# One broadcast DMA in place of two for the rows of B and C of the third channel tile

## What is computed

```python
xz = u @ W_in                                  # 96 -> 2*192 channels
xr, z = split(xz)
x = silu(causal_conv(xr, conv_w) + conv_b)     # 192 channels, 4 taps
dt, B, C = split(x @ W_x)                      # 6 + 16 + 16 columns
delta = softplus(dt @ W_dt + b_dt)
# for every channel d and every state n of 16, along time t:
#   h[t] = exp(delta[t, d] * A[d, n]) * h[t-1] + delta[t, d] * x[t, d] * B[t, n]
#   y[t, d] = sum over n of h[t] * C[t, n]
y = (y + x * D) * silu(z)
out = y @ W_out
```

## Time and profile before

| | before |
|---|---|
| median of 3 runs | 2131.67 us (2131.48 to 2132.75) |
| the profiled execution | 2132.49 us |
| its span, first to last instruction | 2130.5 us |
| GpSimd (POOL) busy | 1938.7 us, 91% |
| VectorE (DVE) busy | 1829.3 us, 86% |
| TensorE (PE) busy | 1819.0 us, 85%, at a mean granted clock of 0.944 |
| DMA | 415.01 MB, the packets of its one busy queue take 64.5% of 16 engines' span |

### The profile page before, as it was taken

One profiled execution on the slowest core, in us unless ns is written; L12 is line 12 of the kernel. 1 busy time (PEld: TensorE's weight loads), 2 busy tenths in 40 slices (PEclk: granted clock), 3 DMA queues, 4 the chain that ended last, 5 costly groups with the idle time before them and its releaser, 6 DMA issues. The chain is left out here.

```text
span 2130.5 us, 16128 instructions
## 1 busy us (share of the span) xinstructions
PE 1819.0 (85%) x4474; PEld 699.1 (33%) x4474; DVE 1829.3 (86%) x1110; ACT 1163.3 (55%) x1206; POOL 1938.7 (91%) x852
## 2 busy tenths in 40 slices
PE   5798789798899899789889889879989988987777
PEld 2233233333333333233333323323333333333322
DVE  2889887877799997997898997998889999799994
ACT  2756464655755745735655744744575574453331
POOL 0999989797899999999999999899899999999996
PEclk9799899999999999999999999999999999989997
DMA  3667556555566776775675785676566677667673
GB/s 83 206 222 185 188 179 189 156 202 189 143 208 204 206 221 205 198 216 191 192 207 197 218 208 204 219 194 211 172 193 208 204 203 217 215 201 213 223 211 94
DMA packets 124454, 415.01 MB, mean 195 GB/s; under 512 B 18556, under 2 KB 22924, under 8 KB 124364
## 3 DMA queue, kind: packets, MB, share of 16 engines
q1 hardware_dynamic: 124364, 413.98, 64.5%
HBM read 403.48 MB, written 6.29 MB: 192 GB/s over the span
## 5 line engine op out<-in xcount | busy, mean ns | idle before, releaser
L861 POOL TENSOR_TENSOR ring<-ring,c_ring 128x1024 f32<-128x1024 f32 x576 | 1344.4, 2355 | 116.9 <-DVE ring L817 104.5
L495 PE MATMUL y_ps<-ring,wp 128*128 128x512 f32 x2304 | 1184.6, 629 | 79.5 <-POOL ring L861 51.0
L817 DVE TENSOR_TENSOR_SCAN ring<-a_ring,b_ps 128x1024 f32<-128x1024 f32 x392 | 895.6, 2285 | 34.1 <-ACT a_ring L624 2.5
L495 PEld LDWEIGHTS y_ps<-ring,wp 128*128 128x128 f32 x2304 | 445.2, 199 | 574.4 <-issue 387.2
L817 DVE TENSOR_TENSOR_SCAN ring<-b_ps,b_ring 128x1024 f32<-128x1024 f32 x184 | 416.6, 2272 | 52.1 <-POOL b_ring L855 24.0
L784 DVE TENSOR_TENSOR b_ps<-u_ab,b_ps 128x1024 f32<-128x1024 f32 x240 | 291.1, 1213 | 101.1 <-PE b_ps L483 88.9
L624 ACT ACTIVATE a_ring<-delta_ab,wp 128x1024 f32<-128x1024 f32 x240 | 271.8, 1140 | 176.9 <-DVE ring L817 176.3
L855 POOL TENSOR_TENSOR b_ring<-u_ab,b_ring 128x1024 f32<-128x1024 f32 x144 | 339.2, 2355 | 0.1
L617 ACT ACT_TABLE_LOAD x186 | 238.6, 1283 | 84.6 <-PE bank L518 36.4
L624 ACT ACTIVATE b_ps<-delta_ab,wp 128x1024 f32<-128x1024 f32 x144 | 160.4, 1115 | 221.2 <-DVE ring L817 220.7
L624 ACT ACTIVATE a_ring<-delta_m,wp 128x1024 f32<-128x1024 f32 x152 | 173.6, 1143 | 152.0 <-DVE ring L817 151.7
(11 more groups left out here) (75 smaller groups left out, 930.4 us busy)
## 6 DMA issues: line engine op xcount, KB each, us to landing
c_ring<-c_rows SPq DMA_DIRECT2D x384, 512.0 KB, 4.4
c_ring<-c_rows SPq DMA_DIRECT2D x384, 256.0 KB, 4.2
b_ring<-b_rows SPq DMA_DIRECT2D x144, 512.0 KB, 5.6
b_ring<-b_rows SPq DMA_DIRECT2D x80, 256.0 KB, 5.3
out<-io SPq DMA_DIRECT2D x16, 192.0 KB, 3.1
io<-x SPq DMA_DIRECT2D x6, 384.0 KB, 6.7
b_in<-parts SPq DMA_DIRECT2D x36, 64.0 KB, 2.1
dt_in<-parts SPq DMA_DIRECT2D x72, 24.0 KB
```

The source lines that it names most:

```text
L495: nc.tensor.matmul(half(y_ps[:, :], j), ident, half(ring[:, g % RING, :], j), start=(n == 0), stop=(n == NS - 1)).then_inc(g_summed, 1)
L817: nc.vector.tensor_tensor_scan(out=h, data0=a, data1=b, initial=0.0, op0=ALU.mult, op1=ALU.add).then_inc(h_ready, 1)
L861: nc.gpsimd.tensor_tensor(r, r, c_ring[:, g % C_RING, :], ALU.mult).then_inc(g_ready, 1)
```

## The change

For the third tile a single `dma_start` takes both batches' rows. Its source is `rows[:, n:n+1, :]` broadcast to the shape [2, 64, 1024], its destination the slot's 128 partitions. Tiles 0 and 1 keep their DMA. The counts on which GpSimd waits fall to 16 per use everywhere.

```diff
-        dmas = lambda g: 2 if g % STEPS // NS == 2 else 1
-        c_uses, spread = [], [0] * C_RING
-        for g in range(ALL_STEPS):
-            spread[g % C_RING] += dmas(g)
-            c_uses.append(16 * spread[g % C_RING])
-        b_uses, spread = {}, [0] * B_RING
-        for m, g in enumerate(pool_steps):
-            spread[m % B_RING] += dmas(g)
-            b_uses[g] = 16 * spread[m % B_RING]
+        c_uses = [16 * (g // C_RING + 1) for g in range(ALL_STEPS)]
+        b_uses = {g: 16 * (m // B_RING + 1) for m, g in enumerate(pool_steps)}
...
             def spread_row(dst, rows, k, n, landed_in):
-                if k < 2:
-                    sp.dma_start(dst, rows[k, n:n + 1, :].to_broadcast([P, T])).then_inc(landed_in, 16)
-                    return
-                for b in range(2):
-                    sp.dma_start(dst[b * DM:(b + 1) * DM, :],
-                                 rows[b, n:n + 1, :].to_broadcast([DM, T])).then_inc(landed_in, 16)
+                src = rows[k, n:n + 1, :].to_broadcast([P, T]) if k < 2 else rows[:, n:n + 1, :].to_broadcast([2, DM, T])
+                sp.dma_start(dst, src).then_inc(landed_in, 16)
```

## The result

| | before | after |
|---|---|---|
| median | 2132.21 us (4 runs) | 3812.28 us (3810.03 to 3819.13, 4 runs) |
| ratio | | 1.7884, 95% interval 1.7853 to 1.7915 |
| span of the profiled execution | 2130.5 us | 3817.3 us |
| twelve third-tile stretches | 760.1 us | 2444.5 us |
| all the rest of the span | 1370.4 us | 1372.8 us |

A stretch is counted as in the prediction, here from GpSimd's timeline: from the end of the product of step 28 to the end of that of step 47. The last three rows are of the two profiled executions (2132.49 and 3819.13 us). Of the 1687 us by which the spans differ, 1684 lie in the stretches; the other parts of the kernel keep their time within 2.4 us.

What follows compares the result with a forecast made beforehand. GpSimd, busy 91% of the span, bounds the kernel before; then two DMA engines pace the third tiles. 2132 + 1687 (232 DMAs at 10.54 us, 2445, less 758) + 35 = 3854, said as 3850 us; range 3600 to 4500.

Steps and rivals of the forecast that it cites:

- The mechanism: Third-tile DMAs: division by outermost dimension, here 2, puts each 512 KB DMA on two fixed engines, 64 rows each; chance 0.80.
- The step that was an extension of the rows: For a DMA whose two sides differ in outermost count, the smaller count decides the engines, here two of 16.
- The price of a row: 4 KB on one engine with a full queue takes 164.7 ns, so a third-tile DMA takes 10.54 us.
- The ends of a stretch: After each of twelve third-tile stretches, landing and last product add 4.4 us, 52 us in all, cancelled against B's earlier issue.
- The time before: The twelve third-tile stretches of the kernel before the change take 758 us in all.
- The small ones: Late `dt_in` loads in item 1 add about 15 us, TensorE's lower clock after the stretches 20 us: 35 us.
- The waits: GpSimd's wait for rows of C grows from 9.1 us to over 1400 us.
- No change: Rival: all 16 engines serve the merged third-tile DMAs, time 2132 us, +-4; chance 0.08.
- faster: Rival: all 16 engines are used and earlier landings remove C waits, -9.1 us at most, 2123 us; chance 0.03.
- The slow price of 271 ns: Rival: two engines, each 4 KB row at the unsaturated stretch's 271 ns, 4024 us in place of 2445, total 5430 us; chance 0.05.
- Rotating pairs: Rival: third-tile DMAs in flight on different engine pairs, about 3 us each, some 2150 to 2500 us; more engines, chance 0.04.

Runs made afterwards that it cites:

- e1: Changed kernel, third-tile rows read from HBM copies, each row 8 times (outermost dimension 16), the item's eight copy writes issued together: 2201.82 us, ratio 1.0329.
- e2: As e1, but with each row 4 times in the HBM copy, so an outermost dimension of 8: 2303.04 us.
- e3: As e1, but with each row twice in the HBM copy, so an outermost dimension of 4: 2664.1 us, ratio 1.2501.
- e7: Changed kernel with each third-tile row as two DMAs, one per half of the time axis, each with outermost dimension 2: 3930.34 us.
- e8: As e1, but with the eight writes of the copies issued one per step over eight steps: 2133.01 us, ratio 0.9994.
- e9: Kernel with only B's third-tile rows merged (2415.19 us), those rows issued nine steps ahead in place of six: 2409.51 us.
- e10: As e2, but with the copies 5 KB apart in HBM in place of 4 KB: 2245.42 us.

## Why the prediction was right

It said 3850 us, the median is 3812; it said +1687 us for the stretches, the trace has +1684.

- **The mechanism.** Right: 11,596 signals, share 0.13, 52 GB/s, and e1, e2 and e3 set the number of engines by the outermost count, with the third tile's bytes the same; e7 brings back the number of DMAs and leaves the engines at two, and the time stays. The step that was an extension of the rows (that the smaller of two unequal counts decides) is now shown for 2, 4, 8 and 16. That the merged rows share one fixed pair is shown by the share of 0.13 with three or four DMAs in flight, 34 us from issue to product ("30 us or more" was predicted).
- **The price of a row.** I took the saturated 164.7 ns; it is 158.9 ns, 10.17 us a DMA and not 10.54, 4% less, and between the two best rows.
- **The ends of a stretch.** Here an error was hidden. 232 x 10.17 = 2359 us, and the stretches take 2444.5, so their ends add 85 us, 7 us each in the mean (some 12 us in a `FWD` item, 1 to 7 in the others); I had set +52 for landing and last product against B's head start and let them cancel. The smaller price and the larger ends offset each other (-86 and +85), so that the sum of 2445 came out to the microsecond by luck. By kind: `FWD` items take 195 to 196 us (190 predicted), `ROWS` 194 to 200 (200), `BWD` 216 to 221 (221).
- **The time before.** 758 us predicted, 760.1 counted.
- **The small ones.** The 35 us for the `dt_in` chain of item 1 and for TensorE's clock are not there: outside the stretches the kernel takes 2.4 us more. The loads of `dt_in` are late as predicted (at 672.6 us TensorE has waited 27.9 us for one), but the first u of the next item is started 2.75 us after GpSimd's last product, where it was 1.00 us before, so the chain costs some 2 us and not 15. TensorE does run at a lower level in the stretches (0.54 granted from 1120 to 1280 us, and 753 ns a matmul at line 484 over the whole kernel against 629 for the same ones before), but no time is lost by it outside the stretches. These terms were wrong, and they are nearly all of the difference between the 3854 worked out and the 3819.13 us of the profiled execution.
- **The waits.** "Over 1400 us" for C: 1417.6, and 250.1 for B, which I had not priced apart. What I had not foreseen is that SyncE's issues themselves are held.
- **The rivals.** No change and faster: both wanted 16 engines, the signals exclude it; e8 shows that on 16 engines "no change" would have been the right one of the two (2133.01, no gain from the 9.1 us of waits). The slow price of 271 ns: not for two engines, so the choice between the two rows was right. The reason given for it, that the row holds pauses, does not hold up: with sixteen engines busy at a share of 0.84 the kernel before has 266 ns, and e2 has 262 ns with eight engines that never rest. What makes a row slow there is open, so nothing on record says why two engines escape it. Rotating pairs: excluded by the steady 10.17 us.

## What to carry to other kernels

Before two DMAs are merged into one, look at the outermost dimension of both sides as they go out, source and destination: a count of 2, 4 or 8 on one side was here the number of DMA engines that worked, and 72 gave 12. A broadcast or a batch dimension in front can leave fourteen of sixteen engines idle without a byte less to move. Count the small packets of the profile against the number of DMAs times 16; that shows engines left out, before any time is compared. And a long transfer on a few engines is not hidden by issuing it early, if transfers that need all engines come behind it in the same queue (e9).

## What was not expected of the hardware

- SyncE's DMA instruction is held when DMAs for the same two engines are queued: 9.97 us for one issue, up to 17.7 us, where it is else mostly 0.32 to 0.6 us. With few engines, the issuing engine becomes a waiting one too.
- The time of 4 KB on one engine is not one number here. With two and four engines it is 159 ns. Eight take 262 ns in some stretches and 164 ns in others of the same execution (e2), and sixteen take 266 ns in a third tile of the kernel before and 161 ns at their best (406 GB/s at a share of 1.02, from 57 to 61 us). With 5 KB between the sources both are still there (e10). The cause is open.
- Cutting rows of 4 KB into rows of 2 KB cost 8 ns for each further row, if the further DMA is counted as free (e7).
- A burst of eight writes of 256 KB in front of the rows on the same queue costs about 6 us an item (e1 against e8).
